# Graph softmax weights ordered by head, direction and key: five transposed tiles of 128 rows for a batch in place of eight of 80

## The reference

```
aff = q_h . k_h / sqrt(32)             # q from all 512 rows, k from rows 0..19
aff = where(label count > 0, aff, NEG) + label_bias
w   = softmax(aff over the 20 keys)
out = out + (w @ sf[:20]) @ Wout[d,h] + bout[d]
x   = x + relu(sf + both directions)
```

## Time and profile before

| what | us |
|---|---|
| median of 3 runs before (lowest, highest) | 1557.32 (1550.26, 1559.01) |
| time of the profiled execution | 1561.64 |
| its span, first to last instruction | 1559.8 |
| PE busy, share of the span | 1346.9 (86%) |
| DVE busy | 925.8 (59%) |
| POOL busy | 903.1 (58%) |
| ACT busy | 629.7 (40%) |
| mean granted TensorE clock | 0.927 of full speed |

### The profile page before, as it was taken

How to read it: one execution, slowest core, us unless ns; L and a number is a source line. 1 busy time by engine, 2 the same in 40 slices (tenths; PEclk the granted TensorE clock), 3 DMA queues, 4 the chain that set the end, 5 groups by cost and what they waited for, 6 DMA issues and landing times.

```text
span 1559.8 us, 19862 instructions
## 1 busy us (share of the span) xinstructions
PE 1346.9 (86%) x5988; PEld 879.0 (56%) x5988; DVE 925.8 (59%) x1496; ACT 629.7 (40%) x1090; POOL 903.1 (58%) x568
## 2 busy tenths in 40 slices
PE   6988898889889853589999999999999999999974
PEld 3646676666667632454565555556555555555532
DVE  3541666676577552266667576667565665756644
ACT  0221323433433333334545545545445445445451
POOL 2003553663574354135658778769578577777793
PEclk9998899999899975779999999999999999999977
DMA  9545221524433323624225343344244253433310
GB/s 298 184 163 146 84 83 65 192 92 138 164 116 116 112 108 143 224 61 119 57 62 149 96 115 103 89 130 116 63 128 107 63 142 96 111 107 87 104 41 28
DMA packets 107192, 179.41 MB, mean 115 GB/s; under 512 B 41312, under 2 KB 50848, under 8 KB 101840
## 3 DMA queue, kind: packets, MB, share of 16 engines
q1 hardware_dynamic: 94976, 143.92, 30.3%
q10 hardware_dynamic: 12112, 34.24, 7.4%
HBM read 81.06 MB, written 46.17 MB: 82 GB/s over the span
## 4 chain that ended last, share of the span: by engine, by line
PE 20%; POOL 17%; issue 8%; DVE 8%; ACT 3%; DMA 1%; SPq 1%; ACTq 1%; POOLq 0%; DVEq 0%
POOL acc L1036 7%; PE a_bank L1458 5%; PE a_bank L1421 4%; DVE rden L1309 4%; POOL acc L1031 3%; PE a_bank L1434 3%; PE a_bank L48 2%; PE a_bank L49 2%; PE a_bank L50 2%; DVE mx L1291 2%; PE a_bank L1469 2%; POOL h L1060 2%; POOL tn L1059 2%; ACT pt L1183 1%; DMA pt<-in_wp_t 1%
## 5 line engine op out<-in xcount | busy, mean ns | idle before, releaser
L1291 DVE TENSOR_REDUCE mx<-a_bank 128x1 f32<-128x512 f32 x512 | 341.6, 674 | 276.1 <-PE a_bank L1434 274.6
L1183 ACT ACTIVATE pt<-a_bank 128x512 f32<-128x512 f32 x512 | 302.3, 597 | 384.3 <-PE a_bank L1421 355.2
L1036 POOL TENSOR_TENSOR acc<-acc,pt 128x1024 f32<-128x1024 f32 x128 | 305.1, 2384 | 18.7 <-ACT pt L1183 10.5
L1421 PE MATMUL a_bank<-sq_stack,sk_stack 98*128 98x512 f32 x512 | 228.7, 449 | 30.8 <-ACT pt L1183 14.9
L1434 PE MATMUL a_bank<-sk_stack,sq_stack 96*128 96x512 f32 x512 | 220.8, 434 | 19.8 <-DVE mx L1291 18.3
L1031 POOL TENSOR_TENSOR acc<-pt 128x1024 f32<-128x1024 f32 x64 | 152.9, 2389 | 118.4 <-PE a_bank L1469 77.6
L1421 PEld LDWEIGHTS a_bank<-sq_stack,sk_stack 98*128 98x128 f32 x512 | 99.1, 194 | 158.5 <-issue 97.8
L788 PE MATMUL g_bank<-m,sf 128*128 128x320 f32 x512 | 149.1, 436 | 1.9 <-issue 1.9
L1434 PEld LDWEIGHTS a_bank<-sk_stack,sq_stack 96*128 96x128 f32 x512 | 100.4, 196 | 67.6 <-DVE mx L1291 53.5
L1309 DVE RECIPROCAL rden<-a_bank 128x128 f32<-128x128 f32 x128 | 119.9, 940 | 21.5 <-PE a_bank L1469 21.5
L48 PE MATMUL a_bank<-hh,wqkh 128*128 128x512 f32 x256 | 105.7, 413 | 29.8 <-DVE wqkl L1379 29.8
(11 more groups left out here) (166 smaller groups left out, 2554.5 us busy)
## 6 DMA issues: line engine op xcount, KB each, us to landing
sq_stack<-qh SPq DMA_DIRECT2D x256, 64.0 KB, 2.0
sk_stack<-kh SPq DMA_DIRECT2D x256, 64.0 KB, 2.1
m_rows<-mout SPq DMA_DIRECT2D x8, 1280.0 KB, 5.0
m<-m_rows SPq DMA_DIRECT2D x8, 1280.0 KB, 5.5
xraw<-in_x_t SPq DMA_DIRECT2D x8, 1024.0 KB, 7.5
xn<-in_x SPq DMA_DIRECT2D x8, 1024.0 KB, 7.4
h_rows<-xn ACTq DMA_DIRECT2D x8, 1024.0 KB, 3.9
t_rows<-houth SPq DMA_DIRECT2D x8, 1024.0 KB, 9.1
```

The source lines that it names most:

```text
L1036: nc.gpsimd.tensor_tensor(acc[:, two, :], acc[:, two, :], pt[:, step + 1, two, :], ALU.add).then_inc(s["sum_done"], 1)
L1183: nc.scalar.activation(pt[:, i, 2 * half + k, :], bank[:, k, :], ACT.Exp).then_inc(s["exp_done"], 1)
L1291: nc.vector.reduce_max(mx[:, half, k, n:n + 1], bank[:, 2 + e % 2, :], AX).then_inc(s["emax_done"], 1)
L1421: nc.tensor.matmul(bank[:, k, :], sk[0:3 * DH + 2, c % 2, j, i * P:(i + 1) * P], sq[0:3 * DH + 2, c % 2, j, :], start=True, stop=True).the ...
```

## The change

The weights in `e` are now laid out by head, direction, key, so 4 heads (a chunk of output) take 160 neighbouring numbers, and the 640 are cut in 5 tiles of 128. Lines 681 and 497 address `e` through a view that puts the direction first; the other users see it as 32 rows of 20 neighbours, as before. A tile meets one or two chunks: `GROUPS` lists the 8 pairs (tile, chunk), which are (0,0), (1,0), (1,1), (2,1), (2,2), (3,2), (3,3), (4,3). Each pair has a 128 x 128 stationary tile in `vdiag` and 3 matmuls, so there are 24 matmuls for a batch as before, with 128 rows in place of 80. Transposes go from 32 of 80 columns to 20 of 128, copies on ACT (587) and differences on DVE (703) from 8 to 5.

`load_v` issues one DMA for each of the 36 `PIECES`: the 32 units of head and direction, of which 4 are cut by a tile's edge. A piece has 20 rows (or 16, 12, 8 or 4 where cut) x 2 parts x 32 numbers. ACT's loops run over 5 tiles, and for tiles 0 to 3 each copy is followed by `scale_ln` and then `hi_chunk` (in the loop after the last step by `scale_ln` and `hi_rows`).

```diff
+TILES = 2 * HK // P
+GROUPS = tuple((k, c) for c in range(FC) for k in range(TILES) if max(k * P, 2 * CK * c) < min((k + 1) * P, 2 * CK * (c + 1)))
+DONE = tuple(sum(1 for k, c in GROUPS if k <= i - 2) for i in range(TILES))
+def pieces():
+    out = []
+    for g, (k, c) in enumerate(GROUPS):
+        row, end = max(k * P, 2 * CK * c), min((k + 1) * P, 2 * CK * (c + 1))
+        while row < end:
+            unit, key = divmod(row, NK)
+            n = min(NK - key, end - row)
+            out.append((g, unit // 2, unit % 2, key, row - k * P, n))
+            row += n
+    return tuple(out)
+PIECES = pieces()
...
-        vdiag = sb("vdiag", [CK, 2, 2, FC, P], F32R)
+        vdiag = sb("vdiag", [P, 2, len(GROUPS), P], F32R)
...
-        e = sb("e", [P, NT, 2, H, NK])
+        e = sb("e", [P, NT, H, 2, NK])
...
-        wth, wtl = sb("wth", [CK, 2, N], F32R), sb("wtl", [CK, 2, N], F32R)
+        wth, wtl = sb("wth", [P, 2, N], F32R), sb("wtl", [P, 2, N], F32R)
...
+        def by_dir(i):
+            return e[:, i].rearrange("p h e k -> p e h k")
+        def by_head(i):
+            return e[:, i].rearrange("p h e k -> p (h e) k")
...
             def load_v(b):
-                for part in range(2):
-                    for dr in range(2):
-                        for j in range(HC):
-                            sp.dma_start(
-                                vdiag[NK * j:NK * j + NK, part, dr, :, DH * j:DH * j + DH].bitcast(F32),
-                                d["v_rows"][part, dr, ds(b * MP, NK), :].rearrange(
-                                    "m (c j g) -> m c j g", c=FC, j=HC)[:, :, j, :]).then_inc(s["v_in"], 16)
+                for g, h, dr, key, row, n in PIECES:
+                    sp.dma_start(vdiag[row:row + n, :, g, DH * (h % HC):DH * (h % HC) + DH].bitcast(F32),
+                                 d["v_rows"][:, dr, ds(b * MP + key, n), h * DH:(h + 1) * DH].rearrange("a m g -> m a g")
+                                 ).then_inc(s["v_in"], 16)
...
             def hi_weights(b, i):
-                act.wait_ge(s["wtr_ready"], 8 * b + i + 1)
-                if i >= 1:
-                    act.wait_ge(s["att_mm"], 8 * b + i - 1)
-                nc.scalar.activation(wth[:, i % 2, :], bank[0:CK, 6 + i % 2, :], ACT.Copy).then_inc(s["wh_done"], 1)
+                act.wait_ge(s["wtr_ready"], TILES * b + i + 1)
+                act.wait_ge(s["att_mm"], 8 * b + DONE[i])
+                nc.scalar.activation(wth[:, i % 2, :], bank[:, 6 + i % 2, :], ACT.Copy).then_inc(s["wh_done"], 1)
...
                 self_features(b, par)
-                for i in range(2 * FC):
+                for i in range(TILES):
                     hi_weights(b - 1, i)
                     if i < FC:
+                        if not (isinstance(b, int) and b == 1):
+                            scale_ln(b - 2, i)
                         if not last:
                             hi_chunk(b + 1, i)
-                    elif not (isinstance(b, int) and b == 1):
-                        scale_ln(b - 2, i - FC)
...
-            for i in range(2 * FC):
+            for i in range(TILES):
                 hi_weights(B - 1, i)
-                if i >= FC:
-                    scale_ln(B - 2, i - FC)
-                    hi_rows(B - 2, i - FC)
+                if i < FC:
+                    scale_ln(B - 2, i)
+                    hi_rows(B - 2, i)
...
-                for i in range(2 * FC + 1):
-                    if i < 2 * FC:
-                        dve.wait_ge(s["wh_done"], 8 * b + i + 1)
-                        nc.vector.tensor_tensor(wtl[:, i % 2, :], bank[0:CK, 6 + i % 2, :],
+                for i in range(TILES + 1):
+                    if i < TILES:
+                        dve.wait_ge(s["wh_done"], TILES * b + i + 1)
+                        nc.vector.tensor_tensor(wtl[:, i % 2, :], bank[:, 6 + i % 2, :],
                                                 wth[:, i % 2, :].bitcast(F32), ALU.subtract).then_inc(s["wl_done"], 1)
-                    if i >= 2 and i % 2 == 0:
-                        c = i // 2 - 1
+                    if i >= 2:
+                        c = i - 2
...
-                for i in range(2 * FC + 1):
-                    if i < 2 * FC:
-                        c, dr = divmod(i, 2)
+                for i in range(TILES + 1):
+                    if i < TILES:
...
-                                bank[0:CK, 6 + i % 2, n * P:(n + 1) * P],
-                                e[:, n, dr, HC * c:HC * c + HC, :].rearrange("p h k -> p (h k)"), t["ident"][:, :].bitcast(F32))
+                                bank[:, 6 + i % 2, n * P:(n + 1) * P],
+                                e[:, n].rearrange("p h e k -> p (h e k)")[:, i * P:(i + 1) * P], t["ident"][:, :].bitcast(F32))
...
                     if i >= 1:
+                        pe.wait_ge(s["wl_done"], TILES * b + i)
+                        for g, (k, c) in enumerate(GROUPS):
+                            if k == i - 1:
+                                if g % 2 == 0 and c >= 2:
+                                    pe.wait_ge(s["att_done"], 4 * b + c - 1)
+                                last = mm3(nc, bank[:, (c + 1) % 2, :], vdiag[:, 0, g, :], vdiag[:, 1, g, :],
+                                           wth[:, k % 2, :], wtl[:, k % 2, :], g % 2 == 0, g % 2 == 1)
+                                last.then_inc(s["att_mm"], 1)
```

More of the change, by code:

```diff
@@ L496, in softmax @@
                         pool.wait_ge(s["mult_done"], 4 * b + i + 1)
-                        nc.gpsimd.tensor_tensor(e[:, i], e[:, i], heads(cadd[:, i]), ALU.add).then_inc(s["add_done"], 1)
+                        nc.gpsimd.tensor_tensor(by_dir(i), by_dir(i), heads(cadd[:, i]), ALU.add).then_inc(s["add_done"], 1)
                     if i >= 2:
@@ L500, in softmax @@
                         pool.wait_ge(s["exp_done"], 4 * b + i - 1)
-                        v = e[:, i - 2].rearrange("p e h k -> p (e h) k")
+                        v = by_head(i - 2)
                         nc.gpsimd.tensor_tensor(v, v, keys(rc[:, i - 2]), ALU.mult).then_inc(s["w_done"], 1)
@@ L535, in _ @@
             front(0)
-            nc.gpsimd.memset(vdiag[:, :, :, :, :].bitcast(F32), 0.0).then_inc(s["set_up"], 1)
+            nc.gpsimd.memset(vdiag[:, :, :, :].bitcast(F32), 0.0).then_inc(s["set_up"], 1)
             label_products(0)
@@ L675, in softmax @@
                 dve.wait_ge(s["adj_step"], 5 * b + 5)
-                dve.wait_ge(s["wtr_ready"], 8 * b)
+                dve.wait_ge(s["wtr_ready"], TILES * b)
                 for i in range(NT + 2):
@@ L680, in softmax @@
                         sc = bank[:, 2 + 2 * (i % 2):4 + 2 * (i % 2), 0:HK].rearrange("p e (h k) -> p e h k", h=H)
-                        nc.vector.tensor_tensor(e[:, i], sc, heads(mask[:, i]), ALU.mult).then_inc(s["mult_done"], 1)
+                        nc.vector.tensor_tensor(by_dir(i), sc, heads(mask[:, i]), ALU.mult).then_inc(s["mult_done"], 1)
                     if i == 0 and has_former:
@@ L684, in softmax @@
                     if 1 <= i <= NT:
-                        v = e[:, i - 1].rearrange("p e h k -> p (e h) k")
+                        v = by_head(i - 1)
                         dve.wait_ge(s["add_done"], 4 * b + i)
@@ L797, in attention @@
                 pe.wait_ge(s["w_done"], 4 * b + 4)
-                pe.wait_ge(s["v_in"], 16 * 16 * b + 16 * 16)
+                pe.wait_ge(s["v_in"], 16 * len(PIECES) * b + 16 * len(PIECES))
                 pe.wait_ge(s["sf_done"], (4 * b + 8) if not isinstance(b, int) else min(4 * b + 8, 4 * B))
-                for i in range(2 * FC + 1):
-                    if i < 2 * FC:
-                        c, dr = divmod(i, 2)
+                for i in range(TILES + 1):
+                    if i < TILES:
@@ L804, in attention @@
                         if i >= 2:
-                            pe.wait_ge(s["wl_done"], 8 * b + i - 1)
+                            pe.wait_ge(s["wl_done"], TILES * b + i - 1)
                         for n in range(NT):
                             last = nc.tensor.transpose(
-                                bank[0:CK, 6 + i % 2, n * P:(n + 1) * P],
-                                e[:, n, dr, HC * c:HC * c + HC, :].rearrange("p h k -> p (h k)"), t["ident"][:, :].bitcast(F32))
+                                bank[:, 6 + i % 2, n * P:(n + 1) * P],
+                                e[:, n].rearrange("p h e k -> p (h e k)")[:, i * P:(i + 1) * P], t["ident"][:, :].bitcast(F32))
@@ L810, in attention @@
                         last.then_inc(s["wtr_ready"], 1)
                     if i >= 1:
[L812 to L818, removed]
@@ L819, in attention @@
-                        last.then_inc(s["att_mm"], 1)
+                        pe.wait_ge(s["wl_done"], TILES * b + i)
[6 more added lines that the diff above has]
+                                last.then_inc(s["att_mm"], 1)
@@ L821, in back @@
             def back(b):
                 pe.wait_ge(s["att_done"], 4 * b + 4)
```

(2 more changed lines are left out.)

## The result

The changed kernel took **1538.14 us** (median of 4 runs, 1531.31 to 1541.06) against 1554.91 for the kernel before (median of 4, 1550.26 to 1559.01): a ratio of 0.987, 95% interval 0.9847 to 0.9892. It is faster by 1.3%, where the prediction said 1566, slower by 0.6%, with 1545 as its low end. The profiled execution of after took 1531.31 us with a span of 1529.4, against 1561.64 and 1559.8 before.

A forecast was written before the change was run, and what follows sets the result against it. A step was taken as PE's own work plus a wait set by DVE and POOL, the start as a chain behind SP's queue. Start +16.3, phases -11.9, last phase +4.5 gave +8.9 us: 1566 us on the median, range 1545 to 1582.

The forecast's parts named there:

- The values load: SP's queue: 36 DMAs at the old price, 0.815 us each outside the loop, 0.95 in it: 29.3 and 34.2 us.
- The lower bound, 0.377 of L116: Values load: the least price considered for an issue, 0.377 us, which L116 takes for 1024 runs.
- The start: Start of the graph stage: x of batch 1 is issued 16.3 us later behind the values, with no slack: +16.3.
- -18.2 by my own working without a stall: Attention phases of batches 0 to 6 if all seven save; the forecast took -11.9, with stalls in batches 3 to 5.
- rival A: Values load: issue goes by runs or is small, 36 take 14.7 us, all phases save; 1545 us, chance 0.20.
- A's point of 0.75 us an issue: Values load: the threshold for rival A, which decides where the 36 issues take under 27 us, 0.75 each.
- The phases: Attention phases: the new order of matmuls and transposes takes 9.8 us in place of 12.48, 2.6 us saved per phase.
- a saving of 1.3 us a phase: Attention phase: the alternative, not followed, that weight loads cost by columns, so the phase saves half of the 2.6.
- The last phase: Last attention phase: ACT's wait for a store moves behind tile 0, with 11.0 us of PE work after it: +4.5.
- over 10 had been named as the sign: Last phase: a PE wait after the first three matmuls (g0) of over 10 us would show the forecast's mechanism.
- The landing doesn't move: Last phase: the store that ACT's first `hi_rows` of batch 6 awaits lands as before, at 583.00.
- the stall behind `xraw`: Phases of batches 3, 4 and 5: x lands late, so PE waits 2.1 us for `wtl`, leaving 0.5 of the 2.6.

The follow-up runs named there:

- b_pad: Kernel before with rows of `v_rows` in HBM 544 numbers apart instead of 512, same 16 DMAs of 80 runs; 1548.64 us in one run, for 1556.6.
- a_fold: Changed kernel with `v_rows` laid out so that key and part are evenly spaced in HBM, same 36 DMAs; 1558.25 us, ratio 1.0014 to the kernel before.
- again: The changed kernel measured once more, unaltered, for a second profile; 1536.69 us against 1556.6, ratio 0.9855.
- a_last: Changed kernel with all five copies of the last batch ahead of batch 6's scalings and roundings on ACT; 1522.65 us, ratio 0.9794.
- a_double: Changed kernel with 32 further cheap DMAs per batch, into a spare tile, ahead of the values; 1549.04 us, ratio 0.9956.

## Why the prediction was wrong

**The values load, the step that failed.** It reads: "the nearest row is L414 itself with the same 20 rows and 128-byte runs at 0.767. I take the same price: 0.815 each outside the loop, 0.95 in it". The measured price is 0.30, and 0.39 and 0.47 from start to start. The row was nearest in its looks only: it shares rows and bytes with the new DMA, but not the pattern on the HBM side, and `b_pad` (0.330) and `a_fold` (0.764) show that this pattern makes the price. The lower bound, 0.377 of L116, was the nearer one. Two terms hang on this step. The start lost 1.0 us, not 16.3, and the loop's `load_first` was issued long before it was due, so no phase stalled: -18.2 by my own working without a stall, not -11.9. With 0.30 put in, the forecast's sum is +1.0 - 18.2 + 4.5 = -12.7, or 1544.6 on the median. That is rival A's figure (1545, chance 0.20) without its first reason, as issue does not go by runs; what decided was A's point of 0.75 us an issue.

**The rest of the way to 1538** is three smaller terms. In the profiles they come to 12.7 us, twice the 6.5 between 1544.6 and 1538.14, so their sizes are those of single executions. *The phases* saved 3.26 us each, not 2.6. Those of batches 2 to 6 take 9.8 us in the mean, the length that the sum gave, and saved 2.9. The phase of batch 0 saved 5.1, as it ran at a granted clock of 1.00 in place of 0.82; that is luck and not foresight (in `again` it took 9.5 us and the phase of batch 1 was the one at full speed, 7.3). A cycle at full speed takes 1.13 us where I had 0.5 + 0.8: the four transposes add 0.35. Against that, the last three matmuls wait 0.26 us for their tile (452.87 to 453.36, for a pace of 0.23), where I had slack. The Trainium skill's rule for weight loads (TensorE: Matmul & The Clock Gate, section LDWEIGHTS (loading the stationary operand)), that their time goes by the number of columns, stood in the prediction with a saving of 1.3 us a phase. The trace doesn't show that proportion for these transposes: the weight loads take 119 ns for 80 columns and 143 for 128 (medians), and eight transposes 1.07 us (459.88 in the earlier trace rows) and 1.09 (440.88).

*The wait before the phase of batch 1*, 5.55 us before and 3.57 now, was not in my sum at all. VectorE and GpSimd ahead of it, in before and then in after:

```profile
237.04 1.15 DVE L665 TENSOR_SCALAR mask<-cnt 128x160 f32<-128x160 f32 x1
238.11 1.30 DVE L667 TENSOR_SCALAR blocked<-cnt 128x160 f32<-128x160 f32 x1
...
236.83 2.48 POOL L482 TENSOR_TENSOR xl<-xraw,xh 128x512 fp32r<-128x512 f32 x2 [1.73 <-ACT xh L554]
```

```profile
232.15 0.23 DVE L688 TENSOR_SCALAR mask<-cnt 128x160 f32<-128x160 f32 x1
232.30 0.24 DVE L690 TENSOR_SCALAR blocked<-cnt 128x160 f32<-128x160 f32 x1
...
232.63 2.88 POOL L506 TENSOR_TENSOR xl<-xraw,xh 128x512 fp32r<-128x512 f32 x2 [2.42 <-ACT xh L578]
```

The same two instructions take 2.45 us where POOL's two subtractions run beside them, each ending 0.1 us behind one of them, and 0.47 where POOL comes later. ACT's new order, with `scale_ln` ahead of `hi_chunk`, moved POOL's start behind them. The Trainium skill (SBUF — State Buffer, section SBUF: two separate sides) says that a shared pair of ports goes to GpSimd or to VectorE for a whole instruction while the other waits, for VectorE in a mode that uses two ports or with two inputs from SBUF. If these two instructions are of that kind, which no run here shows, the trace agrees: 1.15 and 1.30 us for 0.23 and 0.24.

*The last phase* lost 0.2 us, not 4.5. The mechanism is as forecast: PE waits behind the store before the second three (9.88 us idle, over 10 had been named as the sign), and `a_last` gives it back. But that cycle took 12.4 us where I had 15.0, since the store had landed 7.9 us after its issue (547.92 to 555.87), for 10.5 before (572.46 to 583.00). I had said "The landing doesn't move". Beside it the load of `xn` runs, issued 1.3 us ahead of the store before (571.14) and 2.6 now (545.28); that this made the difference is argued, not tried. The last phase of before itself moves by more than 0.2 between executions, as said above. The seven sets of matmuls behind it took 7.9 us for my 9.6, as matmuls ran at full pace from 561.70, 3.9 us in, and not after 7. The transposes behind the phase then found the clock up, the -1.5 of the table.

**Right:** the phase bounds the step and a saving in it comes through whole; the start is a chain with nothing to spare behind SP's queue (`a_double`: 12.57 us in, 12.6 out); and, at the price that I had assumed, the stall behind `xraw` is there (`a_fold`, 1.2 to 1.7 us, for 2.1). Named as a sign in advance: "If the issues take under 0.6 us the forecast is wrong and the kernel is faster."

## What to carry to other kernels

Before a DMA is priced by a row, compare the patterns of both sides, not only bytes and rows: where a load is on the path, a different spacing in HBM can more than halve its issue. When one price carries two terms of a sum, give its other bound the weight of a case of its own. And put the load that the first step waits for ahead of the loads that it doesn't, and the copies that PE waits for ahead of work that waits for a store.

## What the hardware showed that I had not expected

- An issue on SP's queue took 0.30 us for [2,20] runs of 128 bytes and 0.764 once key and part were evenly spaced in HBM; 0.767 for [4,20] and 0.330 once they were not. The number of runs made little difference in the cheap form: in the first load of after the pieces of 4, 8 and 12 rows (8 to 24 runs) took 0.30 to 0.31 and most whole ones 0.33 to 0.35, and `b_pad`'s 80 runs took 0.34 there.
- Two VectorE instructions of 160 elements took 1.15 and 1.30 us beside GpSimd and 0.23 and 0.24 without it.
- The same store of 1 MB landed 7.9 or 10.5 us after its issue, and the load of x 7.5 us after its issue (median of before) or 9.4 with a store of 1 MB beside it (`a_fold`).
